# Row maxima into row 0 of the transposed queries: four small DMAs a group instead of TensorE products and a ScalarE copy

## The reference, cut to what matters

```python
x  = input                          # (2, 2048, 128), float32
xn = layernorm(x)
scores = einsum('bsd,de,bte->bst', xn, qk, xn) / sqrt(128)
scores = where(causal, scores, -inf)
attn   = einsum('bst,btd,de->bse', softmax(scores), xn, ov)
# expert layer on xn: 8 experts, each token goes to argmax(xn @ centroids.T)
#   alpha * (relu(xln @ w1[e] + b1[e]) @ w2[e] + b2[e]), added to xn
out = x + attn + xn + expert part
```

## Time and profile before

| | us |
|---|---|
| median of 3 runs | 235.79 (235.79, 235.79, 237.31) |
| span of the profiled execution | 233.3 |
| TensorE busy | 221.2 (95%) |
| VectorE busy | 177.3 (76%) |
| ScalarE busy | 160.7 (69%) |
| GpSimd busy | 112.4 (48%) |
| SyncE's DMA queue, share of 16 engines | 28.5% |

### The profile page before, as it was taken

One profiled execution on the slowest core, in us unless ns is written; L12 is line 12 of the kernel. 1 busy time (PEld: TensorE's weight loads), 2 busy tenths in 40 slices (PEclk: granted clock), 3 DMA queues, 4 the chain that ended last, 5 costly groups with the idle time before them and its releaser, 6 DMA issues.

```text
span 233.3 us, 7006 instructions
## 1 busy us (share of the span) xinstructions
PE 221.2 (95%) x2542; PEld 173.1 (74%) x2542; DVE 177.3 (76%) x447; ACT 160.7 (69%) x366; POOL 112.4 (48%) x157
## 2 busy tenths in 40 slices
PE   8699999999998999999999999999999999999993
PEld 5464375868777768677548799999998998777672
DVE  6998989888798466889998889766645654458954
ACT  3979999952165997765558645666667667777592
POOL 8648579693047586767300034466546566100000
PEclk9859999999999999999999999999999999999999
DMA  6982511999001111111193001321111111390821
GB/s 183 297 229 91 178 50 42 200 149 139 11 0 57 48 35 48 58 44 50 49 269 86 3 14 37 97 77 34 48 33 51 38 46 45 117 266 7 251 67 45
DMA packets 30960, 20.93 MB, mean 90 GB/s; under 512 B 2088, under 2 KB 28752, under 8 KB 30928
## 3 DMA queue, kind: packets, MB, share of 16 engines
q1 hardware_dynamic: 28320, 15.68, 28.5%
q0 software_dynamic: 2272, 4.67, 6.2%
q10 hardware_dynamic: 336, 0.14, 0.2%
HBM read 11.15 MB, written 9.34 MB: 88 GB/s over the span
## 4 chain that ended last, share of the span: by engine, by line
PE 75%; ACT 13%; DVE 5%; issue 4%; POOL 1%; DVEq 0%; ACTq 0%; POOLq 0%
PE psum L1347 6%; PE psum L1382 5%; PE psum L1348 5%; PE psum L1349 5%; PE psum L1321 5%; PE psum L1391 5%; PE psum L1392 4%; PE psum L1399 4%; PE psum L1496 4%; PE psum L1524 4%; PE psum L1523 4%; PE psum L1522 4%; PE psum L1498 4%; PE psum L1497 4%; DVE row_max L909 2%
## 5 line engine op out<-in xcount | busy, mean ns | idle before, releaser
L685 POOL DMA_INDIRECT sorted_y<-xn,store x39 | 37.3, 958 | 48.3 <-ACT xn L1210 38.6
L1071 ACT ACTIVATE p_sb<-psum 128x512 f32<-128x512 f32 (+1 forms) x80 | 41.9, 538 | 15.3 <-PE psum L1382 15.2
L909 DVE TENSOR_REDUCE row_max<-psum 128x1 f32<-128x512 f32 (+3 forms) x80 | 45.4, 604 | 6.3 <-PE psum L1321 3.7
L675 POOL DMA_INDIRECT sorted_x<-xn,pos x32 | 33.4, 1043 | 24.4 <-DVE pos L845 12.4
L924 DVE TENSOR_TENSOR p_lo<-p_sb,p_hi 128x512 f16<-128x512 f32 (+3 forms) x56 | 33.7, 618 | 14.4 <-ACT p_sb L1071 14.3
L1065 ACT ACTIVATE p_hi<-psum 128x512 f16<-128x512 f32 (+3 forms) x56 | 30.2, 546 | 19.0 <-PE psum L1399 9.0
L1039 DVE SCALAR_TENSOR_TENSOR h_lo<-psum,h_hi 128x512 f16<-128x512 f32 x39 | 26.6, 688 | 13.3 <-ACT h_hi L1203 13.1
L1203 ACT ACTIVATE h_hi<-psum 128x512 f16<-128x512 f32 x39 | 23.3, 597 | 17.8 <-PE psum L1498 17.1
L1347 PE MATMUL psum<-qT_hi,kT_hi 128*128 128x512 f16 (+1 forms) x80 | 27.9, 348 | 1.0 <-ACT p_sb L1071 1.0
L1496 PE MATMUL psum<-x2T,w_hl 128*128 128x128 f16 x156 | 28.0, 220 | 0.2 <-issue 0.2
L1522 PE MATMUL psum<-w_hl,h_hi 128*128 x156 | 28.2, 219 | 0.0
(11 more groups left out here) (209 smaller groups left out, 559.3 us busy)
## 6 DMA issues: line engine op xcount, KB each, us to landing
w_raw<-in_L_ffn_w SPq DMA_DIRECT2D x16, 256.0 KB, 3.3
sorted_x<-zero SPq DMA_DIRECT2D x1, 2515.5 KB, 20.4
xn<-sorted_x SPq DMA_DIRECT2D x8, 258.0 KB, 4.6
x_sb<-in_L_attn_input_data SPq DMA_DIRECT2D x8, 256.0 KB, 6.3
xn<-sorted_y SPq DMA_DIRECT2D x8, 256.0 KB, 5.0
out<-x_sb SPq DMA_DIRECT2D x6, 256.0 KB, 2.6
sorted_y<-xn,store POOLq DMA_INDIRECT x39, 2.2
sorted_x<-xn,pos POOLq DMA_INDIRECT x32, 2.3
```

The lines of the kernel that those rows point to most:

```text
L909: v.tensor_reduce(row_max[:, i, c:c + 1], bank[bank_of[unit]][:, 0:w], AX.X, ALU.max).then_inc(s_max, 1)
L1071: a.activation(p_sb[:, u, off:GW], bank[SCORE[n % R]][:, off:GW], ACT.Exp, scale=SCALE).then_inc(s_exp, 1)
```

## The change

The `SH` job moves from TensorE to SyncE, and `SHa` goes from the list. neg_max becomes two small buffers in turn ([128, 2, 4], float16), and SyncE sends each of its four columns by a DMA of its own from 128 partitions to 128 neighbouring places in row 0 of `qT_hi`. The waits at the first X of a group are for these DMAs. SyncE now has jobs in the list up to SH.1.3, so its wait for the scatters and the first nine loads of sorted rows move to where `SC.31` stands in the list (between SH.1.0 and SH.1.1), and the last two loads to `SO.5` and `SO.8` (between SH.1.2 and SH.1.3). In the list, `W2l.4` with the zero fill stands between SH.0.1 and SH.0.2. Otherwise the list is the same. The banks of the M, T, Q and V jobs shift, as SH takes none.

```diff
-BANKED = ("T", "Q", "V", "W1", "M", "SH", "AFF", "CNT", "INVA")
+BANKED = ("T", "Q", "V", "W1", "M", "AFF", "CNT", "INVA")
...
-        neg_max = sb("neg_max", [P, GT, P], F16)
+        neg_max = sb("neg_max", [P, 2, GT], F16)
...
+        late_loads = {("SO", min(NS, (pairs[-1] + 1) * FT) - SLOTS + 1): pairs for pairs in LOADS if pairs[0] * FT >= SLOTS}
...
+            def send_shift(job):
+                n = nth[job]
+                row = (job[1] * BG + job[2]) * GW
+                sp.wait_ge(s_neg, nth[("RM",) + job[1:]] + 1)
+                sp.wait_ge(s_qlo, job[1] * BG + job[2] + 1)
+                for i in range(GT):
+                    sp.dma_start(qT_hi[0:1, row + i * P:row + (i + 1) * P], neg_max[:, n % 2, i:i + 1],
+                                 allow_slow_non_contiguous=True).then_inc(s_shift[n % 2], 16)
...
-
-            for u in range(SENT):
-                sp.wait_ge(s_sent[u], 16 * len(range(u, NT, SENT)))
-            for pairs in LOADS:
-                load_rows(pairs)
+                if job[0] == "SH":
+                    send_shift(job)
+                if job == ("SC", NT - 1):
+                    for u in range(SENT):
+                        sp.wait_ge(s_sent[u], 16 * len(range(u, NT, SENT)))
+                    for pairs in LOADS:
+                        if pairs[0] * FT < SLOTS:
+                            load_rows(pairs)
+                if job in late_loads:
+                    load_rows(late_loads[job])
...
-                v.wait_ge(s_rm, nth[job] + 1)
-                v.wait_ge(s_fill, 4)
-                wait(v, s_negT, nth[job])
-                v.tensor_scalar(neg_max[:, :, 0], row_m[:], -1.0, SHIFT, ALU.mult, ALU.add).then_inc(s_neg, 1)
+                n = nth[job]
+                v.wait_ge(s_rm, n + 1)
+                wait(v, s_shift[n % 2], 16 * GT * (n // 2))
+                v.tensor_scalar(neg_max[:, n % 2, :], row_m[:], -1.0, SHIFT, ALU.mult, ALU.add).then_inc(s_neg, 1)
...
-            v.memset(neg_max[:], 0.0).then_inc(s_fill, 1)
...
-                if kind == "SHa":
-                    _, b, g = job
-                    k = b * BG + g
-                    a.wait_ge(s_negT, nth["SH", b, g] + 1)
-                    a.wait_ge(s_qlo, k + 1)
-                    a.activation(qT_hi[0:1, k * GW:(k + 1) * GW], bank[bank_of["SH", b, g]][0:1, :], ACT.Copy).then_inc(s_shift, 1)
...
-            def shift(job):
-                at = free_bank(job)
-                pe.wait_ge(s_neg, nth["RM", job[1], job[2]] + 1)
-                for i in range(GT):
-                    m = mm(at[:, i * P:(i + 1) * P], neg_max[:, i, :], ident16[:], start=True, stop=True)
-                m.then_inc(s_negT, 1)
...
                 if j == 0:
                     pe.wait_ge(s_qlo, k + 1)
-                    pe.wait_ge(s_shift, nth["SHa", b, g] + 1)
+                    n_shift = nth["SH", b, g]
+                    pe.wait_ge(s_shift[n_shift % 2], 16 * GT * (n_shift // 2 + 1))
```

More of the change, by code:

```diff
@@ L74 @@
[L74 to L88, removed]
@@ new lines @@
+RN.4.8 MR.0.0.1.0 W1h.2 MR.0.0.2.0 M.0.1.2.0 W2.1 RM.0.0 M.0.1.2.1 M.0.1.3.0 MR.0.1.2.0 W2l.0 W1b.2 MR.0.1.2.1 W1h.3
+M.0.1.1.0 MR.0.1.3.0 W1l.2 M.0.1.0.1 W1b.3 W2l.1 W2.2 W1.4 MR.0.1.1.0 MR.0.1.0.1 ROW.4.8 W1l.3 M.0.1.1.1 SH.0.0
+M.0.1.3.1 W1h.4 W1.5 XA.3 W2l.2 W1l.4 X.0 MR.0.1.3.1 X.1 W1h.5 MR.0.1.1.1 BASE.3 X.2 M.0.1.0.0 EX.0 W1l.5 Q.2 EX.1
+MR.0.1.0.0 BASE.4 P.0 EX.2 Qa.2 XA.5 X.3 Ql.2 M.0.2.1.1 M.0.2.3.1 P.1 RM.0.1 MR.0.2.1.1 M.0.2.3.2 EX.3 BASE.5 P.2 XA.7
+MR.0.2.3.1 M.0.2.0.1 P.3 MR.0.2.3.2 SH.0.1 BASE.6 MR.0.2.0.1 M.0.2.3.0 MR.0.2.3.0 M.0.2.1.2 M.0.2.2.0 W2.3 BASE.7 X.4
@@ new lines @@
+MR.0.2.1.2 MR.0.2.2.0 M.0.2.0.2 M.0.2.0.0 X.5 W2.4 MR.0.2.0.2 W2l.3 MR.0.2.0.0 M.0.2.2.2 M.0.2.1.0 M.0.2.2.1
+MR.0.2.2.2 X.6 W2.5 W2l.4 MR.0.2.2.1 T.3 MR.0.2.1.0 EX.4 COL0 T.4 Ta.3 T.5 R2 EX.5 X.7 W2l.5 QT.0.0.0 EX.6 X.8 W2.6
+QT.0.0.1 X.9 Tl.3 P.4 W2.7 W2l.6 P.5 Ta.4 RM.0.2 W2l.7 Ta.5 T.6 Tl.4 P.6 R2a Tl.5 Ta.6 R2n SH.0.2 EX.7 AFF.0 Tl.6 EX.8
+S.0 T.7 CH.0 Q.3 Ta.7 X.10 Qa.3 X.11 P.7 S.1 Tl.7 EX.9 M.0.3.3.1 Ql.3 M.0.3.2.0 X.12 S.2 MR.0.3.3.1 M.0.3.0.2 P.8
+MR.0.3.2.0 S.3 MR.0.3.0.2 M.0.3.1.1 EX.10 M.0.3.3.3 EX.11 P.9 MR.0.3.1.1 S.4 X.13 MR.0.3.3.3 EX.12 QT.0.1.0 M.0.3.1.2
@@ new lines @@
+X.40 XL.37 EX.39 XL.38 SH.1.1 XL.39 M.1.2.2.0 M.1.2.2.1 PB.37 MR.1.2.2.0 PB.38 PB.39 X.41 EH.40 QT.0.3.0 X.42 EX.40
+M.1.2.1.0 EH.41 MR.1.2.2.1 X.43 M.1.2.1.2 EH.42 XL.40 EX.41 M.1.2.0.1 EX.42 X.44 QT.0.3.1 X.45 MR.1.2.1.0 P.40
+MR.1.2.1.2 P.41 XL.41 M.1.2.2.2 M.1.2.1.1 XL.42 P.42 PB.40 MR.1.2.0.1 PB.41 PB.42 MR.1.2.1.1 M.1.2.0.0 EH.43 EH.44
+QT.1.0.0 P.43 EX.43 EX.44 X.46 MR.1.2.2.2 EH.45 XL.43 M.1.2.3.1 EX.45 XL.44 X.47 MR.1.2.3.1 X.48 XL.45 PB.43 W1.6
+EH.46 QT.1.0.1 EX.46 TU.0 P.44 W1h.6 XL.46 P.45 TUa.0 PB.44 W1l.6 PB.45 X.49 TUl.0 EH.47 W1.7 MR.1.2.0.0 EX.47 RM.1.2
@@ new lines @@
+YS.7 TU.10 LO.17 OUT.16 RE.18 HI.19 TUa.10 SO.11 LO.18 OUT.17 TUl.10 RE.19 OUT.18 SO.12 YS.8 LO.19 TU.11 HI.20 SO.13
+TUa.11 HI.21 RE.20 TUl.11 OUT.19 SO.14 RE.21 TU.12 LO.20 HI.22 YS.9 LO.21 M.1.3.0.2 SO.15 TUa.12 OUT.20 RE.22
+MR.1.3.0.2 HI.23 TUl.12 SO.16 OUT.21 RM.1.3 RE.23 LO.22 HI.24 SO.17 TU.13 LO.23 OUT.22 RE.24 HI.25 TUa.13 LO.24 YS.10
+OUT.23 TUl.13 RE.25 SH.1.3 OUT.24 YS.11 LO.25 SO.18 HI.26 TU.14 OUT.25 RE.26 SO.19 HI.27 TUa.14 LO.26 YS.12 SO.20
+TUl.14 RE.27 OUT.26 LO.27 TU.15 SO.21 HI.28 TUa.15 OUT.27 SO.22 RE.28 TUl.15 HI.29 YS.13 TU.16 LO.28 HI.30 RE.29
@@ L160, in build @@
     N_EARLY = 8
-    N_FILL = 6
+    N_FILL = 5
     N_WARM = 24
@@ L376, in build @@
         s_neg = sem("s_neg")
-        s_negT = sem("s_negT")
-        s_shift = sem("s_shift")
+        s_shift = [sem(f"s_shift{u}") for u in range(2)]
         s_sc = sem("s_sc")
@@ L1442, in work @@
                     max_unit(job)
-                if kind == "SH":
-                    shift(job)
                 if kind == "X":
```

95 lines of the change are left out of this document (43 added, 52 removed).

## The result

The changed kernel takes **283.77 us** (median of 4 runs, 283.46 to 284.19), the kernel before 236.55 beside it (4 runs, 235.79 to 238.23): a ratio of 1.196, 95% interval 1.191 to 1.201. Slower was forecast, but the 260.8 us, and the upper end of the range at 268, were too low: the loss is 47 us, not 25. Some executions of a kernel come out some per cent slower whatever the kernel; the ratios in this document leave them out, so a ratio need not be the quotient of the two medians beside it.

What follows compares the result with a forecast made beforehand. TensorE was taken as the bound, busy 221.2 of 233.3 us. Stalls of 10.2 and 11.8 plus 3.4 for the clock, less 0.4 for products, gave +25.0: span 258.3, plus 2.5 around it, 260.8 us; range 248 to 268.

Steps and rivals of the forecast that it cites:

- Both collisions: SyncE's queue: group 0.2's shifts land behind the zero fill, 10.2 us; group 1.1's behind scatters and loads, 11.8 us.
- the general price: Each group's four DMAs on SyncE: about 3.4 us from neg_max ready to shifts landed, mostly within the groups' slacks.
- From the landing of the fill to the score product: Group 0.2: fill lands at 60.8, the small DMAs' own work adds 1.2 us, release at 62.0.
- packets rose by 4608: Sign named for the profile: packets under 512 B up from 2088 by 32 x (128 + 16) = 4608.
- Added, in general: Step pricing each group's four SyncE DMAs: 3 x 0.35 + 2.3 = 3.4 us; stalls only 0.4 in 0.1, 1.8 in 0.3.
- if a landing in an idle queue takes over 5 us: Sign that would show the forecast wrong, for small DMAs on SyncE; landings near 2 to 4 expected in 0.3 and 1.0.
- rival of dear elements: 2-byte elements cost 4 us more at each of the two releases, 0.2 and 1.1: 268.8 us, chance 0.12.
- first rival: Small DMAs overtake the fill at group 0.2; 1.4 us remain from 0.0 and 0.1, 1.1 stalls 10.2: 248.7 us, chance 0.12.
- This wait swallows the losses of groups 0.0 and 0.1: TensorE's 10.2 us wait at group 0.2, behind the fill, was said to absorb earlier losses and gains there.
- plus or minus 1: Start of the zero fill on SyncE: up to 1 us earlier or later than in the kernel before.
- the clock, 3.4 us: TensorE runs at a lower clock after each of two long stalls, 1.7 us each, from a range of nothing to 3.3.
- Group 1.1: Shifts issued only after SyncE's scatter wait and loads, landing at 126.3 against a score product at 114.48: 11.8 us stall.

Runs made afterwards that it cites:

- e12: Changed kernel with one transfer of 8-byte chunks per group instead of four columns (queries get another's maximum): 261.41 us, ratio 1.107 to the kernel before.
- e6: Kernel before with the DMA path for groups 0.2 and 1.1 only, SyncE's wait and loads moved as in the change: 302.02 us, ratio 1.074.
- e10: Kernel before with the DMA path for groups 1.2 and 1.3 only: 234.67 us against 235.46, ratio 0.996.
- e9: Kernel before with eight kinds of small scratch transfers on SyncE after the fill: four columns into one row 7.3 us, one transfer of 8-byte chunks 1.9.
- e7: Kernel before with the DMA path for groups 0.0, 0.1, 0.3 and 1.0 only: runs from 286.75 to 295.65 us, too far apart for a ratio.
- e14: Changed kernel with one transfer per group (another query's maximum), fill issued behind group 0.2's shifts and loads behind group 1.1's: 234.35 us, ratio 0.992 to the kernel before.
- e13: Changed kernel with the fill issued behind group 0.2's shifts and the loads behind group 1.1's, run on a 236 us chip: 259.63 us, ratio 1.098.
- e4: Changed kernel with products of zeros keeping TensorE busy in five of its stalls: 308.67 us, ratio 1.098 to the kernel before.
- e2: Changed kernel with the zero fill issued by ScalarE on its own DMA queue, at the same job: 308.26 us, ratio 1.090 to the kernel before.
- e8: Changed kernel with the fill issued behind group 0.2's shifts and the loads behind group 1.1's, on a 282 us chip: 294.69 us, ratio 1.049.

## Why the prediction was wrong, point by point

**Right: what bounds, and the two places.** TensorE was the bound, and a stall before 195 us came out at the end nearly in full (47.6 us at group 1.1, 49.0 at the end). Both collisions came where forecast. e12 comes near the forecast's kernel: its stalls are 10.7 and 11.2 us (forecast 10.2 and 11.8), its release at 63.3 (forecast 62.0), and its time is 261.4 (forecast 260.8). It confirms the two collision terms and not the general price, as one transfer takes 1.9 us there and not the forecast's 3.4; that the totals agree so closely is in part luck, since two small waits (1.9 us) and the removed products (1.8 us, of which the forecast counted 0.4) cancel. The small transfers waited for all but the end of the fill, and were not let in between its rows: in e6 the first of them landed at 63.0, 18.8 us after its issue and 1.1 ahead of the fill, the last behind it. From the landing of the fill to the score product, 1.2 us in the forecast, measured 1.5, and 0.3 to 2.2 in the other traces; packets rose by 4608 as worked out; groups 1.2 and 1.3 cost nothing (e10).

**Wrong: "Added, in general", 3.4 us.** This is the step that failed first: it measured 7.3. I gave the four transfers the issue time of 128-row loads (0.35 us; 0.60 measured) and one landing of 2.3 us for all four, as if they flew side by side; the first did land after 2.7, and each further one came about 1.5 us later. Group 0.0 lost a little more, since SyncE came to it only at 27.57, behind loads of weights (neg_max was there at 24.8): its slack of 4.7 us counted from neg_max was 1.8 from the queue. In place of 0, 0.4, 1.8 and 0 us of stall, groups 0.0, 0.1, 0.3 and 1.0 had 5.9, 4.5, 6.2 and 1.0. The prediction named this itself as what would make it wrong, "if a landing in an idle queue takes over 5 us", and its rival of dear elements priced it at two releases only. In its first rival, the 1.4 us said to remain from 0.0 and 0.1 do not follow from the general price either, which gives 0.4 there. Why four columns take 7.3 us stays open: e9 shows that it isn't their elements alone and isn't a fixed time per transfer.

**Wrong: "This wait swallows the losses of groups 0.0 and 0.1", with the fill "plus or minus 1".** A wait swallows an earlier delay only if its release stays where it is. The fill is issued at W2l.4, behind weight loads that wait for GpSimd's part of the weight copies; this waits for ScalarE's part, which stands behind its score jobs, and those wait for the stalled products (ScalarE idles 6.37 us for one of them, up to 36.95). So the fill moved 8.4 us (8.8 in e7), and group 0.2's stall of 9.4 us came on top of 12.9 already lost. The same holds for 0.3 and 1.1: the first scatter started at 92.29 against 67.19 in the trace of before, the nine loads at 146.88 against 115.26. The 32 scatters start over 51.9 us, where they take 44.4 in e12, whose stall at 0.3 is 0.9 us instead of 6.2: the scatters are held up by that stall too, and nothing was swallowed. The landing of the fill, 20.4 us, lay between 19.1 and 25.2 over the traces, which added 4.8 us here. I don't know the cause of this spread; the DMA engines' share was down to 0.01 from 72 to 74 us, with the fill still to land.

**Right for two falls, too few falls: the clock, 3.4 us.** From e14 to e12 the two long stalls add 3.7 us of busy TensorE time from 28.5 us on, where the forecast had 3.4, the middle of a wide range, so with some luck; from e14 to e13 the short ones add 8.0. (Over the whole span it is 5.0 and 9.6, but 1.3 and 1.6 of that lie in the start.) I had counted none for the short stalls, which the general price made no stalls at all. That the low clock lengthens the work behind a short stall is shown at the first, by 2.4 us (e4); for the others it is read off the granted clock (0.70 in the second window above).

**Group 1.1.** 15.0 us against 11.8: the shifts' issues took 4.3 us behind the loads instead of 1.4, and they landed 5.0 to 6.1 us after their issues.

## What to carry to other kernels

Price a set of small DMAs from its issue to its last landing, and don't give each the landing of one: bytes that can go as one transfer of longer chunks should (7.3 against 1.9 us). Before a later wait is said to swallow an earlier delay, follow what its release itself waits for; if it goes back to the delayed engine, the losses add. And a value that is needed soon should stand ahead of bulk transfers in issue order: another queue did not carry it past the fill (e2), an earlier place did (e8, e13).

## What the runs showed of the hardware that was not expected

- With the engines full of the fill, one issue on the same queue took 6.25 us in the changed kernel and 9.91 in e12; on the other queue 0.6.
- A stall of 5.9 us was followed by 8.5 us of full work at a mean granted clock of 0.72; the same 4.1 us of work took 6.5 behind it.
- The same program took 236 us on some chips and 282 on others, with waits shown as "remote" of up to 21.9 us; the loss from one and the same change was 47 us on the first and 31 on the second.
- Four transfers of 128 two-byte elements took 3.7 us where source and destination partitions were the same, 6.2 to 7.3 where each went from 128 partitions into one row.
- A zero fill of 2.5 MB took 19.1 to 25.2 us in kernels that differ little.
